# Dequantising by four parametric Relus, turning the tokens by transposing DMAs, an opening without GpSimd library calls, and unrolled loops, in a one-core SSM + NF4 FFN block

## What is computed

```python
x = L0_attn_u                                   # (4, 512, 512) float32
xn = _layernorm(x, axis=-1)
# convolution branch
K = _s4_kernel(Lambda, p, q, B, Ct, step, L)
y = irfft(rfft(xn, n=2*L) * rfft(K, n=2*L), n=2*L)[..., :L] + D[0] * xn
# FFN branch, M = 1792, BLOCK = 64
w = NF4_CODE[q.reshape(-1)].reshape(-1, BLOCK) * absmax[:, None]     # for each of gate, up, down
g, u = xn @ Wg.T, xn @ Wu.T
out = x + y + (silu(g) * u) @ Wd.T
```

## Time and profile before

| | us |
|---|---|
| median of 3 runs | 524.62 (523.37 to 525.79) |
| span of the profiled execution | 522.3 |
| PE busy | 480.9 (92%) |
| DVE busy | 368.4 (71%) |
| ACT busy | 323.3 (62%) |
| POOL busy | 34.1 (7%) |
| first product starts (L955) | 44.22 |
| PE without idle time from | 68.91 |
| last matmul ends | 519.15 |

### The profile page before, as it was taken

How to read it: one execution, slowest core, us unless ns; L and a number is a source line. 1 busy time by engine, 2 the same in 40 slices (tenths; PEclk the granted TensorE clock), 3 DMA queues, 4 the chain that set the end, 5 groups by cost and what they waited for, 6 DMA issues and landing times.

```text
span 522.3 us, 7842 instructions
## 1 busy us (share of the span) xinstructions
PE 480.9 (92%) x2316; PEld 228.7 (44%) x2316; DVE 368.4 (71%) x643; ACT 323.3 (62%) x525; POOL 34.1 (7%) x118
## 2 busy tenths in 40 slices
PE   0039989999999999999999999999999999999997
PEld 0025534444444444444444464456544444444443
DVE  2568798878778787989779997989999991200013
ACT  7149897878787877777777766885599970000000
POOL 0064740000000000000000000000000000000000
PEclk9999999999999999999999999999999999999999
DMA  7514111111111111121212110245422300400003
GB/s 253 191 37 121 42 40 61 47 56 54 47 57 43 60 40 60 41 61 40 62 40 62 40 55 31 57 135 183 147 97 84 99 21 8 153 0 0 0 27 135
DMA packets 19572, 36.42 MB, mean 70 GB/s; under 512 B 3488, under 2 KB 3680, under 8 KB 19168
## 3 DMA queue, kind: packets, MB, share of 16 engines
q1 hardware_dynamic: 19552, 36.17, 22.2%
HBM read 31.97 MB, written 4.19 MB: 69 GB/s over the span
## 4 chain that ended last, share of the span: by engine, by line
PE 87%; issue 5%; ACT 3%; POOL 2%; DVE 2%; POOLq 0%; ACTq 0%
PE bank L955 53%; PE bank L1069 28%; PE bank L1052 5%; POOL h L313 2%; ACT h L470 1%; ACT xT L475 1%; PE bank L942 1%; ACT line L414 1%; PE bank L1031 1%; DVE h L666 1%; DVE xT L676 0%; DVE acc_r L559 0%; DVE xT L930 0%; DVE acc_l L555 0%; ACT h L462 0%
## 5 line engine op out<-in xcount | busy, mean ns | idle before, releaser
L955 PE MATMUL bank<-xT,w 128*128 128x512 f16 x1344 | 292.7, 380 | 2.0 <-DVE xT L676 1.4
L414 ACT ACTIVATE line<-qs,lb 128x512 f32<-128x512 int32 x328 | 214.9, 712 | 15.6 <-DVE acc_l L555 5.3
L955 PEld LDWEIGHTS bank<-xT,w 128*128 128x128 f16 x1344 | 131.8, 98 | 161.1 <-issue 4.0
L1069 PE MATMUL bank<-wd,h 128*128 (+1 forms) x672 | 145.2, 379 | 0.0
L1069 PEld LDWEIGHTS bank<-wd,h 128*128 (+2 forms) x672 | 65.7, 98 | 79.1
L611 DVE SCALAR_TENSOR_TENSOR bank<-bank,sc,sil 128x512 f32<-128x512 f32 x56 | 42.4, 756 | 40.6 <-PE bank L955 40.4
L462 ACT ACTIVATE h<-bank 128x512 f32 (+1 forms) x56 | 33.4, 596 | 53.3 <-DVE bank L611 53.3
L930 DVE SCALAR_TENSOR_TENSOR xT<-bank,sc,xT 128x512 f32<-128x512 f32 x16 | 11.4, 748 | 77.3 <-PE bank L1069 77.3
L564 DVE TENSOR_TENSOR acc_r<-acc_r,line 128x512 f32<-128x512 f32 x82 | 56.2, 686 | 0.7 <-ACT line L414 0.7
L564 DVE TENSOR_TENSOR acc_l<-acc_l,line 128x512 f32<-128x512 f32 x82 | 56.2, 686 | 0.0
L942 PE MATMUL bank<-ident,h 128*128 128x128 f32 x64 | 13.0, 355 | 36.3 <-ACT h L470 35.9
(11 more groups left out here) (71 smaller groups left out, 149.5 us busy)
## 6 DMA issues: line engine op xcount, KB each, us to landing
w<-in_x SPq DMA_DIRECT2D x16, 256.0 KB, 3.5
out<-xT SPq DMA_DIRECT2D x16, 256.0 KB, 2.0
qs<-in_q_gate SPq DMA_DIRECT2D x14, 256.0 KB, 2.6
qs<-in_q_up SPq DMA_DIRECT2D x14, 256.0 KB, 2.6
am<-in_am_gate SPq DMA_DIRECT2D x28, 128.0 KB, 2.9
am<-in_am_up SPq DMA_DIRECT2D x28, 128.0 KB, 2.9
qs<-in_q_down SPq DMA_DIRECT2D x14, 256.0 KB, 2.6
am<-in_am_down SPq DMA_DIRECT2D x28, 128.0 KB, 2.9
```

The costliest lines, as they stand in the source:

```text
L414: nc.scalar.activation(line_of(seq, k), qs[:, slot, :], ACT.Identity, scale=slope, bias=lb[:, k:k + 1]).then_inc(line_done, 1)
L955: mm = nc.tensor.matmul(out_b[:], w1[:, par, unit, wl, f, :], xT[:, TPC * c:TPC * c + TPC, xl, f, :], start=(n == 0), stop=(n == 3 * NC - 1))
L1069: mm = nc.tensor.matmul(bank[(t + 4) % 8][:], part, wd[:, mt, wl, :], start=(isinstance(mt, int) and mt == 0 and n == 0), stop=(isinstance ...
```

## The change

It does five things.

- **Dequantising.** In place of eight lines a unit has four *knees*: ACT applies a parametric Relu to the codes (`make_knee`; scale, bias and the slope below zero are immediates), and DVE combines them in five steps. A unit costs ACT 5 instructions in place of 9 and DVE 6 in place of 9.
- **Turning.** The normalised tile is split first, in SBUF, and in the order of the tokens: ACT copies the high half (`x_hi`, into `xst`), POOL subtracts for the low half (`x_lo`, 16 instructions of 128x512), and SP issues one transposing DMA of 128x1024 fp16 for each tile (`turn`) into `xT`. The 64 transposes on PE, and ACT's and DVE's copies out of PSUM, are gone. PE waits for the four DMAs of a chunk (`xt_ld`).
- **Opening.** POOL's identity and its first all-reduce are gone. The identity is a comparison of two loaded rows on DVE, the maximum over partitions one transpose and one small matmul on PE with a reduce and a copy on DVE, and 1/sqrt is made by DVE in 13 small steps (`rstd`). DVE also normalises the first chunk. ACT's queue issues four of the first loads.
- **Order.** PE's first eight products are (0,0), (0,1), (1,0), (1,1), (0,2), (0,3), (1,2), (1,3) in place of the four of tile 0 and then those of tile 1. `b_cp`, ACT's copy of the S4 vector, stands ahead of the fourth. SP's loads of codes and scales are placed between the turns; in the last stage the down units' loads stand in other places (`XR_DOWN`), and the last window has 22 items of DVE and 19 of ACT.
- **Loops.** All are unrolled.

```diff
+OPENING = [(0, 0), (0, 1), (1, 0), (1, 1), (0, 2), (0, 3), (1, 2), (1, 3)]
+ORDER = OPENING + [(k, c) for k in range(2, NM) for c in range(NCH)]
...
+NF4_KNEES = [
+    (0.13015560805797577, -0.1608591079711914, 2.334184408187866),
+    (0.09105004370212555, -0.4834947884082794, 1.0946502685546875),
+    (0.0918029397726059, -0.8843734264373779, 0.8861361742019653),
+    (0.2770431637763977, -3.8099708557128906, 0.44002941250801086),
+]
...
+KNEE = ACT.Prelu
+
+STEPS = 5
+KNEES = 4
+ACT_ITEMS = KNEES + 1
+DVE_ITEMS = STEPS + 1
+ACT_AHEAD, DVE_AHEAD = 8, 6
+XR_DOWN = (4, 8, 12)
+LAST_ITEMS = 22
...
+        def dq_after(u, s):
+
+            if u < 2:
+                return 2 * u + s + 1 if s < 2 else 3 + 3 * u + s
+            return STEPS * u + s + 1
...
+            def load_codes(u, q_src):
+
+                if u >= 2:
+                    sp.wait_ge(knee_done, KNEES * (u - 1))
+                sp.dma_start(qs[:, u % 2, :], q_src).then_inc(q_ld[u % 2], 16)
+
+            def load_absmax(u, am_src):
+                if u >= 2:
+                    sp.wait_ge(dq_done, dq_after(u - 2, 4))
...
+            def turn(t):
+
+                sp.wait_ge(xlo_done, t + 1)
+                sp.dma_start_transpose(xT[:, t].rearrange("p l c f -> p (l c) f"),
+                                       xst[:, t % 8].rearrange("p l d -> p (l d)")).then_inc(xt_ld[t // TPC], 16)
...
+            load_codes(2, q_gate[1])
+            load_codes(3, q_up[1])
+            for t in range(0, 4):
+                turn(t)
+            load_absmax(2, am_gate[1])
+            load_absmax(3, am_up[1])
+            sp.dma_start(cols[:], s4_cols).then_inc(s4_ld, 16)
+            sp.dma_start(vcs, vct).then_inc(s4_ld, 16)
+            sp.dma_start(bps, bp).then_inc(s4_ld, 16)
+            load_codes(4, q_gate[2])
+            for t in range(4, 8):
+                turn(t)
+            load_absmax(4, am_gate[2])
+            load_codes(5, q_up[2])
+            for t in range(8, 12):
+                turn(t)
+            load_absmax(5, am_up[2])
+            for t in range(12, 16):
+                turn(t)
...
-            for mt in range(4):
-                load_down(mt, mt % 2)
+            for mt in range(6):
+                load_down(mt)
             for t in range(NT):
                 if t < 4:
 
-                    sp.wait_ge(up_done, NCH * (NM - 1 + t // 2))
+                    sp.wait_ge(up_done, LAST_USE[NM - 2 + t // 2] + 1)
                 else:
                     sp.wait_ge(res_done, t - 3)
                 sp.dma_start(xr[:, t % 4, :], x_v[:, t, :]).then_inc(xr_ld[t % 4], 16)
-                if t in (3, 12):
-                    load_down(4 + t // 12, t // 12)
-            with sp.Fori(DOWN_LOOP, NM - 1, 2) as mt:
-                for par in range(2):
-                    load_down(mt + par, par)
+                if t in XR_DOWN:
+                    load_down(6 + XR_DOWN.index(t))
+            for mt in range(6 + len(XR_DOWN), NM):
+                load_down(mt)
...
-            pool.memset(ident[:], 0.0).then_inc(id_done, 1)
-            pool.wait_ge(id_done, 1)
-            pool.affine_select(out=ident[:], in_=ident[:], compare_op=ALU.not_equal, fill=1.0, base=0,
-                               pattern=[[-1, P]], channel_multiplier=1).then_inc(id_done, 1)
-            pool.wait_ge(sc_done, 1)
-            pool.partition_all_reduce(amax, amx[:, 0:3], P, bass.bass_isa.ReduceOp.max).then_inc(mx_done, 1)
...
-                for _ in range(3):
-                    rs_next(pool.tensor_tensor, t, y, y, ALU.mult)
-                    rs_next(pool.tensor_tensor, t, t, hv, ALU.mult)
-                    rs_next(pool.tensor_scalar, t, t, 1.5, None, ALU.add)
-                    rs_next(pool.tensor_tensor, y, y, t, ALU.mult)
...
+            pool.memset(one3, 1.0).then_inc(one_done, 1)
+            pool.memset(warm, 1.0).then_inc(one_done, 1)
+            pool.wait_ge(one_done, 2)
+            pool.tensor_tensor(warm, warm, warm, ALU.subtract).then_inc(one_done, 1)
+
+            def x_lo(t):
+                pool.wait_ge(xhi_done, t + 1)
+                pool.tensor_tensor(xst[:, t % 8, LO, :], xnb[:, t % 8, :], xst[:, t % 8, HI, :],
+                                   ALU.subtract).then_inc(xlo_done, 1)
+
+            for t in range(NT):
+                x_lo(t)
...
-                slope = NF4_LINES[k][0]
-                nc.scalar.activation(line_of(seq, k), qs[:, slot, :], ACT.Identity, scale=slope,
-                                     bias=lb[:, k:k + 1]).then_inc(line_done, 1)
...
+                scale, bias, below = NF4_KNEES[k]
+                nc.scalar.activation(knee_of(u, k), qs[:, u % 2, :], KNEE, scale=scale, bias=bias,
+                                     alpha=below).then_inc(knee_done, 1)
...
+                nc.scalar.activation(xst[:, t % 8, HI, :], xnb[:, t % 8, :], ACT.Copy).then_inc(xhi_done, 1)
...
+            items(10, 17)
+            norm(4)
...
+            norm(8)
+            norm(9)
+            x_hi(8)
+            norm(10)
+            x_hi(9)
+            norm(11)
+            x_hi(10)
+            x_hi(11)
+            act.wait_ge(b_mm, 1)
+            nc.scalar.activation(yv[:, 0:2], bank[7][:, 0:2], ACT.Copy).then_inc(b_cp, 1)
+            silu(2)
...
+            norm(12)
+            norm(13)
+            x_hi(12)
+            silu(3)
+            norm(14)
+            x_hi(13)
+            norm(15)
+            x_hi(14)
+            x_hi(15)
+            h_hi(3)
+            silu(4)
...
+                per = 10 if k < NM - 1 else 19
...
+            def step(u, s):
+                left, right = sides_of(u)
+                whole = whole_of(u)
                 if s == 0:
-                    dve.wait_ge(line_done, made + 2)
-                    ins = nc.vector.scalar_tensor_tensor(acc_l[:], line_of(seq, 0), NF4_PIVOT, line_of(seq, 1),
-                                                         ALU.min, ALU.min)
+                    dve.wait_ge(knee_done, KNEES * u + 2)
+                    ins = v.scalar_tensor_tensor(left, knee_of(u, 0), LEFT_STEP, knee_of(u, 1), ALU.add, ALU.min)
                 elif s == 1:
-                    dve.wait_ge(line_done, made + 4)
-                    ins = nc.vector.tensor_tensor(acc_r[:], line_of(seq, 2), line_of(seq, 3), ALU.max)
-                elif s < 6:
-                    dve.wait_ge(line_done, made + 3 + s)
-                    dve.wait_ge(dq_done, STEPS * seq + s - 1)
-                    acc, op = ((acc_l, ALU.min), (acc_r, ALU.max))[s % 2]
-                    ins = nc.vector.tensor_tensor(acc[:], acc[:], line_of(seq, 2 + s), op)
-                elif s == 6:
-                    dve.wait_ge(dq_done, STEPS * seq + 6)
-                    ins = nc.vector.scalar_tensor_tensor(wt[:], acc_r[:], -NF4_PIVOT, acc_l[:],
-                                                         ALU.max, ALU.add)
+                    dve.wait_ge(knee_done, KNEES * u + 4)
+                    ins = v.scalar_tensor_tensor(right, knee_of(u, 3), RIGHT_STEP, knee_of(u, 2), ALU.add, ALU.max)
+                elif s == 2:
+                    dve.wait_ge(dq_done, dq_after(u, 1))
+                    ins = v.tensor_scalar(right, right, RIGHT_FLOOR, RIGHT_SHIFT, ALU.max, ALU.add)
+                elif s == 3:
+                    dve.wait_ge(dq_done, dq_after(u, 2))
+                    ins = v.scalar_tensor_tensor(whole, left, LEFT_TOP, right, ALU.min, ALU.add)
                 else:
-                    dve.wait_ge(am_ld[slot], 32 * loads)
-                    dve.wait_ge(dq_done, STEPS * seq + 7)
-                    ins = nc.vector.scalar_tensor_tensor(wt[:], wt[:], s_w[s_scale], am[:, slot, :],
-                                                         ALU.mult, ALU.mult)
+                    if u == 0:
+                        dve.wait_ge(sc_done, SCALES)
+                    dve.wait_ge(am_ld[u % 2], 32 * (u // 2 + 1))
+                    dve.wait_ge(dq_done, dq_after(u, 3))
+                    which = 2 if u >= GU else u % 2
+                    ins = v.scalar_tensor_tensor(whole, whole, s_w[which], am[:, u % 2, :], ALU.mult, ALU.mult)
                 ins.then_inc(dq_done, 1)
...
+                elif s == 1:
+                    dve.wait_ge(mx_tp, 1)
+                    small(v.tensor_reduce, mx3, bank[7][0:3, 0:P], AX.X, ALU.max)
+                elif s < 5:
+                    exponent(s - 2, mx3, pw3[:, 0:1], pw3[:, 1:2])
+                elif s < SPREAD:
+                    i = s - 5
+                    small(v.tensor_scalar, dg3[:, 3 * i:3 * i + 3], ident[0:3, 0:3], pw3[:, i:i + 1], None, ALU.mult)
+                elif s == SPREAD:
+                    dve.wait_ge(mx_bc, 1)
+                    small(v.tensor_copy, sc[:, 28:34], bank[7][:, P:P + 6])
...
+            def rstd(c, i):
+
+                a, b = TPC * c, TPC * c + TPC
+                var, hv, y, p, r = mv[:, a:b, 1], rs[:, 0, a:b], rs[:, 1, a:b], rs[:, 2, a:b], rs[:, 3, a:b]
+                if i == 0:
```

(53 more changed lines are left out.)

678 lines of the change are left out of this document (313 added, 365 removed).

## The result

The changed kernel takes 538.25 us (median of 4 runs, 537.98 to 538.76), the kernel before 524.0 in the same comparison: ratio 1.0267 [1.0243, 1.0292]. The forecast was 526.5, within 516 to 538.

The account below looks back on a forecast made before the run. PE was taken to bound from 68.91 to 519.15 us. 522.3 - 5.0 (opening) + 1.7 (half rate) + 4.1 (late seams) = 523.1; with bias 524.6, with 2.3 from span to median 526.9, rounded to 526.5; range 516 to 538.

Parts of the forecast that it names:

- What bounds, and the yardstick: PE bounds from 68.91 to 519.15; kernels compared at five products done, 79.3 before, leaving 443.0 us.
- A clock below 9 in any slice: Sign of being wrong: the granted clock of PE reading below 9 anywhere in the profile.
- Dequantising: 42 units lose 120 us of ACT and 86 us of DVE; worth nothing behind 79.3; a knee taken as 0.62 us.
- Prelu: Rival: knees on ACT dearer than Identity; +0.2 us each gives 530, +0.6 gives 540; chance 0.06.
- Unrolling: All loops: no gain on PE, cost taken as 0, from -0.5 to +1.
- First product, 27.1: Opening: DVE's work bounds, identity's row at 7.4; PE's first product starts at 27.1 against 44.22.
- Waits at the second, fourth and sixth product: Opening: PE waits 7.2, 3.6 (for `b_cp`) and 6.1 us; sixth product starts at 74.3, 5.0 us early.
- Half rate: PE idling at the opening's seams brings the half rate back once more, +1.7 us.
- Late seams, 4.1: PE waits 2.3 us at the convolution's fifth tile and 1.8 at the fifth down tile, together +4.1.
- the bias of 1.5: Added to the sum: the same method put the kernel before 5.7 us too quick, of which 1.5 stays.
- the dear transposing DMA: Rival: sixteen transposing DMAs in one queue at 2.5 us each give 538; decides from about 1.5; chance 0.22.
- Quick turns without late waits: Rival: turned tiles land 2.0 us after issue, no late seams or renewed half rate; time 518, chance 0.22.

Follow-up runs that it names:

- experiment 4: The kernel before with every loop written out as straight code and nothing else changed: 523.12 us against 523.78, ratio 0.9991.
- experiment 6: The changed kernel with ACT's queue issuing the identity's row and column ahead of 768 KB of input and codes: 539.05 us, ratio 1.029 to the kernel before.
- experiment 7: The changed kernel with the identity's loads first and SP holding the second chunk's 1 MB load until the up unit's codes landed: 534.1 us, ratio 1.0206.
- experiment 10: The changed kernel with five moves of order together, among them identity's loads first, `b_cp` sooner and input reloads issued by GpSimd: 524.04 us, ratio 1.0001.
- experiment 9: The changed kernel with the low halves of the first chunk's four tiles made by DVE in place of GpSimd: 537.13 us, ratio 1.0253.
- experiment 3: The changed kernel with input reloads issued by GpSimd and 16 DVE and 15 ACT items in the last window: 527.56 us, ratio 1.0063.
- experiment 1: The changed kernel with the ninth down unit's load issued behind all sixteen input reloads, not behind the thirteenth: 531.04 us, ratio 1.0129.
- experiment 8: The changed kernel with each transposing DMA replaced by a plain copy of the same 256 KB, tokens not turned: 535.36 us, ratio 1.0207.
- experiment 11: The changed kernel with combined order moves, the second chunk's load held back, and the third and fourth chunks' 1/sqrt moved on DVE: 520.37 us, ratio 0.9933.
- experiment 5: The changed kernel with DVE computing the fourth chunk's 1/sqrt ahead of the third product's `h_mul`: 538.24 us, ratio 1.0262.

## Why the prediction was right, and where not

The time lay a quarter of a microsecond above the range's end; "slower" had the largest of the three chances, 0.46, but the number given was a small difference, and a clear loss came. By the steps of the prediction:

- **What bounds, and the yardstick:** right. From the sixth product on the matmuls take 0.216 us where nothing stops them, and both kernels can be compared there. A clock below 9 in any slice was named as a sign of being wrong, and it came: the rate was lower behind the waits of PE at the seams.
- **Dequantising:** the sizes were right (a knee 619 ns on the page of after, 0.62 taken; DVE busy 291.3 us, 77 less), and so was its worth. Prelu isn't dear: that rival is out.
- **Unrolling:** 0, right (experiment 4).
- **First product, 27.1:** measured 31.26. The step that failed is the load of the identity's row, taken as 7.4 between 4.5 and 11.5; its column landed at 12.8, later than my upper end, and DVE's `rstd` ended at 20.8 for 17.1, 3.7 of the 4.2 us. I had counted the loads ahead of it and none of those beside it in the other queue (experiments 6 and 7). GpSimd's 1.23 us a tile (1.2 taken, on average over all sixteen; 1.33 in this chunk) and the turn's landing of 3.3 (3.8 taken) were close, its issue of 1.33 (1.2 taken) too.
- **Waits at the second, fourth and sixth product:** 7.8, 3.0 and 4.2 us for 7.2, 3.6 and 6.1, and the first product itself took 8.5 for 6.9. Each was where it was forecast, with the instruction that was named; that the fourth waits for `b_cp` is shown by experiment 10, where the copy stood ahead and the wait was gone. The sixth product came at 79.63 for 74.3: the 4.2 us from the start, and DVE slowed by GpSimd, which I had not thought of, 2.1 us in the first chunk alone (experiment 9). Part of that chain is hidden in the shorter third wait.
- **Half rate:** +1.7 forecast for one seam; 2.6 there, and 1.6 more behind the down wait (144.19 for 660 matmuls, where 0.216 each would be 142.6), which is part of the next term.
- **Late seams, 4.1:** the wait at the fifth tile of the convolution was 2.44 for 2.3, right in size, place and cause (experiment 3: with fewer items ahead it vanishes; a late reload has a share of some 0.3 in it). The other one was mis-sized: 1.8 forecast, 0.77 + 5.57 and the slow matmuls behind it measured. I had named its cause ("the input tiles are now behind loads of units that wait themselves") and got its size wrong: SP stood at the ninth unit's scales until 379.75 and held back reloads whose buffers had been free for up to 4.2 us. The landing is not what was off, 3.9 us for 3.5 taken: in experiment 1 a reload takes 4.1 us to land, and with the one load out of the way there is no wait. This is the largest term of the error, 7.0 of 11.7 us (536.3 measured for 524.6): 11.1 in the last stage for 4.1. The opening is 5.3 and the clock 0.9; against these stands the bias of 1.5, which I had added for just such an error of the opening and which was too small for it.
- **The rivals:** 538 was the dear transposing DMA's number, and the time is there by coincidence. Its mechanism is refuted: 1.33 us an issue is under its 1.5 us threshold, and all sixteen cost about 3 us (experiment 8). Its argument from the small-packet load of 6.2 us did not hold. Quick turns without late waits, 518, needed the order of experiment 11.

Of the rules that the prediction weighed, that of the Trainium skill ("GPSIMD Engine Reference", "Elementwise — side-by-side cycle accounting"), GpSimd at about twice DVE's time, gets 1229 ns for 685 here, 1.8 times. The 1.0 us of data time estimated from the Trainium skill ("DMA: Bandwidth & Descriptors", "Latency and other measured facts") can't be separated in the trace: the landing of a turn is 1.0 us above that of a plain copy of the same bytes.

What stays open: why the clock comes back sooner in one run than in another with the same instructions (the second product at 0.64 to 0.77), which makes up most of the opening's spread of 1.4 us; why the last wait varies between 3.2 and 5.6 us where the last stage is unchanged; and what of experiment 8's gain there is the plain copy's.

## What to carry to other kernels

A queue that issues both loads on the critical path and loads that wait for a slower engine is a chain: when work is moved, read for each wait in it what is queued behind, with the landing time measured in that stage, and give the urgent loads a queue of their own. A faster step in an opening is worth what arrives at the first engine that then never stops; put all loads, queues and engines side by side up to that point, since each relief here met the next bound within a microsecond or two. In the first microseconds the loads that another queue issues beside a load delay it as well as those ahead of it.

## What the runs showed of the hardware

- GpSimd slows DVE when both work from SBUF: 0.42, 0.69 and 0.75 us became 1.00, 1.52 and 1.42 with GpSimd's subtraction beside them, and single steps of 128x4 took 1.0 us for 0.16 (experiments 5 and 11). The Trainium skill ("SBUF — State Buffer", "Who interferes with whom") says that a DVE instruction with two inputs in SBUF contends with a GpSimd one that reads SBUF, and that in a two-port mode whichever comes second waits for the whole of the other; the rows agree, the steps of 1.0 us above all, which stood beside subtractions of 1.2 us. It spoke against this change, and I had missed it.
- A transposing DMA of 256 KB takes SP 1.33 us to issue and lands in 3.3 us, a plain one 0.48 and 2.3 (experiment 8).
- A 256 KB load from ACT's queue landed in 11.9 us beside SP's loads and in 7.6 with those held back (experiments 6 and 7).
- After PE had idled 4.2, 4.4 and 5.6 us the granted clock was at its lower level for the next matmuls (0.50 from 79 to 83 us in the changed kernel), and 1.4 to 2.6 us were lost each time. After 3.4 us it cost 1.5 (experiment 11); after some 3.0 us 1.8 in the changed kernel and nothing in experiment 5; after 1.4 nothing (experiment 11).
